# Position bias: the first layer's evictions as operations of 1024 columns over two PSUM banks

## The reference

```python
pos = grid_q[:, :, None, :] - grid_kv[:, None, :, :]
bias = jnp.sign(pos) * jnp.log1p(jnp.abs(pos))
bias = jax.nn.relu(bias @ cpb_w1 + cpb_b1)
bias = jax.nn.relu(bias @ cpb_w2 + cpb_b2)
bias = (bias @ cpb_w3 + cpb_b3).reshape(b, GROUPS, H * W, Hd * Wd)
sim = jnp.einsum('bhid,bhjd->bhij', qh, kh) + bias
```

## Time and profile before

| | us |
|---|---|
| median of 3 runs | 4650.07 |
| lowest, highest | 4640.69, 4652.29 |
| the profiled execution | 4645.78 |
| its span, first to last instruction | 4644.0 |
| mean granted TensorE clock | 0.946 |
| busy PE, PEld | 4177.0, 2352.9 |
| busy DVE, ACT, POOL | 2894.8, 2530.4, 990.1 |

### The profile page before, as it was taken

The page is one execution under the profiler, slowest core; times in us unless marked ns, Lnnn a source line. Parts: engine busy times, 40 slices in busy tenths (PEclk is TensorE's granted clock), DMA queues, the critical chain, the costliest instruction groups (busy, mean ns, idle before and its releaser), DMA issues. The chain is left out here.

```text
span 4644.0 us, 65947 instructions
## 1 busy us (share of the span) xinstructions
PE 4177.0 (90%) x19516; PEld 2352.9 (51%) x19516; DVE 2894.8 (62%) x4078; ACT 2530.4 (54%) x4526; POOL 990.1 (21%) x684
## 2 busy tenths in 40 slices
PE   2599999999999999999989997769989977878988
PEld 1355555555555555555567775234444443344443
DVE  7877777777777777777773333556766533244442
ACT  3588888888888888888864332111221210112221
POOL 1401111011111111011105445022222100035553
PEclk7799999999999999999999998889999978989999
DMA  1200000000000000000020000387666412442211
GB/s 42 84 2 2 2 2 2 2 2 2 2 2 2 2 2 2 2 2 2 2 74 1 0 0 14 125 332 261 235 214 232 168 43 79 155 100 50 61 37 73
DMA packets 97301, 280.43 MB, mean 60 GB/s; under 512 B 33120, under 2 KB 34144, under 8 KB 78016
## 3 DMA queue, kind: packets, MB, share of 16 engines
q0 software_dynamic: 20736, 151.00, 9.2%
q1 hardware_dynamic: 76480, 128.39, 9.1%
HBM read 224.38 MB, written 54.85 MB: 60 GB/s over the span
## 5 line engine op out<-in xcount | busy, mean ns | idle before, releaser
L572 DVE SCALAR_TENSOR_TENSOR cpb_r<-cpb_z,cpb_r 128x512 fp32r<-128x512 f32 x2052 | 1321.8, 686 | 491.8 <-ACT cpb_r L547 486.0
L547 ACT ACTIVATE cpb_r<-cpb_z 128x512 fp32r<-128x512 f32 x2052 | 1121.2, 605 | 277.7 <-PE cpb_z L479 277.7
L553 ACT ACTIVATE cpb_h<-cpb_z,net_vec 128x512 f32<-128x512 f32 x1536 | 1020.5, 714 | 2.0 <-PE cpb_z L495 2.0
L492 PE MATMUL cpb_z<-cpb_r,cpb_w2a 128*128 128x512 f32 x2048 | 856.7, 418 | 3.0
L493 PE MATMUL cpb_z<-cpb_r,cpb_w2b 128*128 128x512 f32 x2048 | 803.5, 392 | 0.0
L495 PE MATMUL cpb_z<-cpb_r,cpb_w2a 128*128 128x512 f32 x2048 | 797.3, 389 | 0.0
L430 POOL TENSOR_TENSOR cpb_exp<-l0k_posx,l0k_pos 128x1024 bf16 (+1 forms) x130 | 247.4, 1903 | 1966.1 <-PE cpb_z L479 1947.0
L1322 PE MATMUL dc_pc<-dc_sc,l_dcw 128*128 128x512 f32 x1152 | 533.7, 608 | 6.5 <-ACT dc_dc L1377 6.5
L492 PEld LDWEIGHTS cpb_z<-cpb_r,cpb_w2a 128*128 128x128 f32 x2048 | 384.1, 188 | 189.8 <-issue 123.3
L504 PE MATMUL cpb_zo<-cpb_h,cpb_w3w 128*32 128x512 f32 x3584 | 477.3, 605 | 0.0
L495 PEld LDWEIGHTS cpb_z<-cpb_r,cpb_w2a 128*128 128x128 f32 x2048 | 385.3, 188 | 85.2
(11 more groups left out here) (318 smaller groups left out, 4542.2 us busy)
## 6 DMA issues: line engine op xcount, KB each, us to landing
corners<-cf_tt SPq DMA_DIRECT2D x77, 256.0 KB, 3.6
qk_parts<-gn_r SPq DMA_DIRECT2D x64, 256.0 KB, 2.0
l_dcw<-in_dc_wT SPq DMA_DIRECT2D x9, 1024.0 KB, 10.9
bias_dram<-cpb_bst SPq DMA_DIRECT2D x520, 8.0 KB
net_x<-in_x SPq DMA_DIRECT2D x8, 1024.0 KB, 8.8
sa_qa<-qk_parts SPq DMA_DIRECT2D x16, 512.0 KB, 9.2
sa_ka<-qk_parts SPq DMA_DIRECT2D x16, 512.0 KB, 11.2
l_w<-in_mlp_w1T SPq DMA_DIRECT2D x1, 4096.0 KB, 23.7
```

Source lines behind the costliest of these rows:

```text
L492: pe.matmul(z2[:, bank, :], W2A[:], R1[:, k, :], start=True, stop=False)
L547: act.activation(R1[:, t % RING, :], z1[:, t % 4, :], ACT.Relu).then_inc(r1_ready, 1)
L553: act.activation(H2[:, t % 8, :], z2[:, t % 3, :], ACT.Relu, bias=V("cpb_b2")).then_inc(h2a, 1)
L572: v.scalar_tensor_tensor(R2[:, t % RING, :], z1[:, t % 4, :], 0.0, R1[:, t % RING, :].bitcast(F32), ALU.max, ALU.subtract).then_inc(r2_rea ...
```

## The change

The first parts and second parts of two neighbouring tiles become one instruction each. ACT's relu reads 1024 columns over two banks of `z1` and writes two neighbouring tiles of `R1`; DVE's operation does the same for `R2`. The semaphores go up by 2 at the end of each, and DVE waits for both tiles (`t + 2`) instead of the first (`t + 1`). The second layer, `hidden`, the third layer and all buffers stay. Lines behind the edit move by one (L572 becomes L571, L598 becomes L597, L578 becomes L577).

```diff
--- before.py
+++ after.py
@@ -541,10 +541,10 @@
 
         @block.scalar
         def _(act):
-            def first_part(i, t):
+            def first_parts(i, t):
                 if t % 4 == 0:
                     act.wait_ge(z1_ready, i * QUADS + t // 4 + 1)
-                act.activation(R1[:, t % RING, :], z1[:, t % 4, :], ACT.Relu).then_inc(r1_ready, 1)
+                act.activation(R1[:, t % RING:t % RING + 2, :], z1[:, t % 4:t % 4 + 2, :], ACT.Relu).then_inc(r1_ready, 2)
 
             def hidden(i, t):
                 act.wait_ge(z2_ready, i * TPI + t + 1)
@@ -552,25 +552,24 @@
                     act.wait_ge(h2_free, i * QUADS + t // 4 + 1)
                 act.activation(H2[:, t % 8, :], z2[:, t % 3, :], ACT.Relu, bias=V("cpb_b2")).then_inc(h2a, 1)
 
-            for t in range(4):
-                first_part(0, t)
+            for t in range(0, 4, 2):
+                first_parts(0, t)
             act.sem_inc(h2a, FREE)
             with act.Fori(0, ITERS) as i:
                 for t in range(0, TPI, 4):
-                    first_part(i, t + 4)
-                    first_part(i, t + 5)
+                    first_parts(i, t + 4)
                     hidden(i, t)
-                    first_part(i, t + 6)
-                    first_part(i, t + 7)
+                    first_parts(i, t + 6)
                     hidden(i, t + 1)
                     hidden(i, t + 3)
 
         @block.vector
         def _(v):
-            def second_part(i, t):
-                v.wait_ge(r1_ready, i * TPI + t + 1)
-                v.scalar_tensor_tensor(R2[:, t % RING, :], z1[:, t % 4, :], 0.0, R1[:, t % RING, :].bitcast(F32),
-                                       ALU.max, ALU.subtract).then_inc(r2_ready, 1)
+            def second_parts(i, t):
+                k = t % RING
+                v.wait_ge(r1_ready, i * TPI + t + 2)
+                v.scalar_tensor_tensor(R2[:, k:k + 2, :], z1[:, t % 4:t % 4 + 2, :], 0.0, R1[:, k:k + 2, :].bitcast(F32),
+                                       ALU.max, ALU.subtract).then_inc(r2_ready, 2)
 
             def read_out(i):
                 v.wait_ge(h2_free, i * QUADS + 2)
@@ -587,12 +586,12 @@
             for c in range(8):
                 v.tensor_copy(W3W[:, c, c:c + 1], V("cpb_w3")).then_inc(win_ready, 1)
             v.sem_inc(h2v, FREE)
-            for t in range(4):
-                second_part(0, t)
+            for t in range(0, 4, 2):
+                second_parts(0, t)
             with v.Fori(0, ITERS) as i:
                 for t in range(0, TPI, 4):
-                    for k in range(4):
-                        second_part(i, t + 4 + k)
+                    for k in range(0, 4, 2):
+                        second_parts(i, t + 4 + k)
                     v.wait_ge(z2_ready, i * TPI + t + 3)
                     v.wait_ge(h2_free, i * QUADS + t // 4 + 1)
                     v.tensor_scalar(H2[:, (t + 2) % 8, :], z2[:, (t + 2) % 3, :], V("cpb_b2"), 0.0, ALU.add, ALU.max
```

## The result

| | before | after |
|---|---|---|
| median of 4 runs | 4645.38 us | 4736.98 us |
| profiled execution's span | 4644.0 us | 4735.6 us |
| ratio, 95% interval | | 1.0198 [1.0178, 1.0218] |

The change makes the kernel 2% slower. I had forecast 4653 us, no change, with a range to 4700; it came out 84 us above the forecast and close to what my first rival gave as its upper end (4747), but, as the rows show, not for the reason given there.

What follows compares the result with a forecast made beforehand. PE was taken to bound the stage at 4.27 us a quad. The new loop's terms also summed to 4.27, a tie; 0.006 us in each of 512 quads added 3 us to 4650.07, giving 4653 us, range 4638 to 4700.

Steps and rivals of the forecast that it cites:

- my first rival: Eviction loop outlasts PE; with wide ACT 1.09 and wide DVE 1.29 us, 0.19 over, 4747 us; chance 0.23.
- That PE bounds the quad, with a loop 0.29 us ahead of it: Position bias stage: PE's own period is 4.27 us a quad; the eviction loop through ACT and DVE runs 0.29 ahead.
- The lengths, 1.03 and 1.22 us: Wide 1024-column operations: 1.03 us on ACT (L547), 1.22 us on DVE (L572), from slopes of other rows.
- Sum 0.45 + 0.91 + 0.57 + 1.07 + 1.22 + 0.05 = 4.27 us: New loop from one L479 to the next through ACT and DVE, equal to PE's own period of 4.27 us.
- first and fourth term: L479 to ACT's first pair, 0.45 us; second pair on ACT to its DVE operation, 1.03 + 0.04 = 1.07.
- In the opening quad ... a reserve of 0.30 after the 0.05, which covers the added 0.29: Quad opening an iteration: DVE ends at 1216.15, L479 comes at 1216.50, so the longer loop should still fit.
- Rival 1: Loop outlasts PE if the second wide L572 ends later than 4.22 us after L479; every 0.01 over is 5 us; chance 0.23.
- Rivals 2 and 3: 2: the 0.34 us DVE-to-PE hand-over stays, 4798 us, chance 0.03; 3: eviction throughput bounds the quad, 4589 us, chance 0.04.

Runs made afterwards that it cites:

- The narrow kernel with 0.13 us more in its loop: Kernel before, every operation still narrow, but each L547 and L572 adds 2 to its semaphore and waits are doubled: 4650.81 us, ratio 1.0021.
- the fastest version: Kernel before, with DVE taking the relu of tile 29 instead of 30 in each iteration's last quad: 4636.27 us, ratio 0.9981.
- the edge edit: DVE takes tile 29's relu instead of tile 30's in each iteration's last quad; on the change: 4725.33 us, ratio 1.0175 to the kernel before.

## Why the prediction was wrong

- **That PE bounds the quad, with a loop 0.29 us ahead of it: right.** The narrow kernel with 0.13 us more in its loop keeps its 4.27. The releaser's name in the waits view was misleading before and is misleading still in the fastest version, where the loop has its full reserve:

```profile
PEld cpb_z L479 <- DVE cpb_r L572: 353.8, 422, 0.8
```

- **The lengths, 1.03 and 1.22 us: right** to a hundredth (1.028, 1.225), from rows of other operations. For ACT there was some luck in it: the two rows that gave the slope aren't of one kind, L242 is a relu with a scale and a constant bias, L1385 a square. Advanced Engine Details and Errata, The Read-Write Bubble, in the Trainium skill had one expect that larger tiles lose less between instructions. The traces agree: a pair on DVE went from 1.29 to 1.225 us, on ACT from 1.09 to 1.03. It bought nothing, as neither engine bounds the quad.
- **"Sum 0.45 + 0.91 + 0.57 + 1.07 + 1.22 + 0.05 = 4.27 us": this step failed, in its first and fourth term.** I carried the two hand-overs over unchanged. The diff also changes what the operations add, from 1 to 2, and I gave that no price. It costs 0.06 us in the first term (PE to ACT) and 0.06 to 0.07 in the fourth (ACT to DVE, inside its 1.07), since each of these waits becomes an instruction of its own. With 1 instead of 2 the sum holds: 4.28. As the sum was a tie, the whole error fell on the quad: 65 of the 92 us.
- **"In the opening quad ... a reserve of 0.30 after the 0.05, which covers the added 0.29": wrong.** I looked at L479 and not at the first L492 behind it. Two things stand there that occur once in eight quads: a bank that DVE frees last, and PE's turn of the loop, 0.24 us, which the reserve had hidden. Rows 7 showed the opening quad 0.10 longer than the rest before, and I used that number to close a check without asking what it was. That was the hint. It cost 27 us; the wide kernel that adds 1 still pays 23 of them (64 x 0.355). Of the change's 27, the edge edit takes back 64 x 0.18 = 12.
- **Rival 1, slower by a loop that outlasts PE: the right mechanism**, and its place and its "0.01 us over is 5 us" hold (0.146 over, 65 us in 448 quads). Its price was worked out from longer operations, which didn't come. I put it at 0.23 and cut the range at 4700.
- **Rivals 2 and 3: refuted** by the 0.06 us from DVE's end to L479, and by ACT and DVE having 61 and 66 us less to do at a longer time.
- **That spending the whole reserve on a change which can gain nothing is a poor trade** stood in the sum. With PE as the bound the best case was zero; every term forgotten could only count against it. The chances should have said so.

## What to carry to other kernels

When two operations are merged, let the merged one still add 1 and count in pairs at the waits: here the addition of 2 alone cost 65 us of 4737. Even so the merged kernel stayed 0.6% slower than the one before. A reserve that a change consumes also hid things that no view lists, such as the loop's turn and the one tile whose bank is freed late at an iteration's edge; look for the quad that is different before, and ask what makes it so. If the gain is off the bound, a forecast of "a tie" should be read as "slower or the same".

## What the runs showed of the hardware that I had not expected

- An operation that adds 2 to a semaphore starts later behind its wait than one that adds 1: 0.11 against 0.05 us on ACT behind PE, 0.10 against 0.03 on DVE behind ACT (medians over the trace), whatever its width. With 2 the wait ahead of the operation is an instruction of its own in the sequencer's records (513 on ACT and 1026 on DVE with the change), with 1 there is none.
- The cost of a loop's turn on PE depends on how early its last wait is met: 0.23 us when the wait is met as the engine falls free, 0.08 when it is met 0.16 earlier, none at 0.29. The branch itself takes 0.21 us and starts 0.15 after DVE's end in all three.
- A read of 1024 columns over two PSUM banks is not slower per column than one of 512: 1.028 us against 0.605, so 0.423 for 512 more columns, where two SBUF rows of before, of different functions, gave 0.427.
